# Where the second key head of the context is turned, and what ScalarE evicts around the scores

## The chip, the cores and the metric

The kernel runs on one core of one Trainium2 chip. The metric is the device time of one execution in microseconds (us). TensorE (PE) multiplies and also turns tiles by multiplying with an identity matrix, VectorE (DVE) reduces and normalises, ScalarE (ACT) evicts PSUM banks and takes exponentials, GpSimd (POOL) does elementwise work in SBUF, and SyncE (SP) issues the DMAs.

## The reference

One transformer block in float32 on `x` (8 batches of 112 tokens, 512 channels) with a context of 8 x 375 rows. The part that the change touches is the attention:

```python
ln_out = _ln(hidden_states, ln_w, ln_b)
q  = _ln(fp8_linear(ln_out, wq)).reshape(b, s, g, hpg, d)    # 16 heads, 8 key heads, d = 128
k  = _ln(fp8_linear(ln_out, wk)); v = fp8_linear(ln_out, wv)
core = _gqa(q, k, v)                                         # softmax(q k^T / sqrt(d)) v
qx = _ln(fp8_linear(ln_out, wqx))
kx, vx = split(einsum('bsi,oi->bso', cond, w_kv_x))          # cond: the context
kx = _ln(kx)
xout = _gqa(qx, kx, vx)                                      # 112 queries against 375 context rows
```

The two outputs are concatenated, quantised and projected, and a layer of experts follows, which the change does not touch.

## The kernel before

The weights of the projections are split into 4 groups (`GP`) of four query heads and two key heads. For each group the kernel goes over the 8 batches, so there are 32 attentions, numbered here t = 0 to 31. Each step of the order in `passes` (L399) projects a batch `s` and, interleaved with it, does the attention of the batch before it, `t`. Queries and own keys are projected for 128 rows at a time, so 7 of 8 batches carry such a tile ("has a tile") and the eighth only projects its own values and its context. The context of a batch is projected in three blocks of 125 rows, `project(s, 3)` to `project(s, 5)`, each 12 matmuls: four with the high halves `c_hi`, `w_hi`, four with `c_lo`, `w_hi`, four with `c_hi`, `w_lo`.

Every engine has its order written out by hand in a function `step`, and one called `last_step` for the batch without a tile. That gives five kinds of steps with an attention in them:

- plain steps, 20 of them (t = 4, 5, 8 to 13, 16 to 21, 24 to 29)
- steps that also round inputs on VectorE (`rounding`, L1043), 4 of them (t = 0 to 3, in the first group)
- last steps (`last_step`), 4 of them (t = 6, 14, 22, 30); in the first three VectorE also splits weights of the next group (`w_low`)
- first steps of a new group (`change == "new"`), 3 of them (t = 7, 15, 23)
- the attention of the last batch alone, 1 (t = 31)

A step in TensorE's order: the projections `project` 0 and 1, `turn` 0 to 2 (own queries, cross queries, own keys), `turn(t, 3)` (first key head of the context), `project` 2, `score_self`, `score_cross` 0 and 1, `turn(t, 4)` (second key head of the context), `project` 3, `turn_self` (L845), `turn_cross` 0 (L852), `score_cross` 2, `turn_cross` 1, `score_cross` 3, `project` 4, outputs, `turn_cross` 2 and 3, `project` 5, outputs. `turn_self` and `turn_cross` turn the probabilities; `turn_cross` 1 writes the PSUM bank that `turn_self` wrote, so it waits until VectorE has copied that bank out in `take_self` (L1121).

ScalarE: `c_high(s, k)` (L581) rounds a block of the context to `c_hi`; `turned(t, n)` (L640 for the context's keys) evicts a turned bank; `take(s, j)` evicts a projection; `exp_self` (L656) and `exp_cross` (L664) take the exponentials. GpSimd: `c_low(s, k)` (L529) computes `c_lo = c_raw - c_hi`, 128x500 float32 in SBUF, as soon as `c_high(s, k)` is done; `rstd(s, j)` (L516, L523) follows each. VectorE: `max_self` (L1093), `max_cross` (L1107), `norm_self` (L1101), `norm_cross` 0 and 1 (L1115, a tensor_scalar in SBUF), `take_self` (L1121), and later `scale(s, 5)` (L1087), which normalises the last block of the context's keys. SyncE reloads `c_raw` for block k when `c_high` and `c_low` of it are done.

Of the kernel before, what the change touches and what calls it, by code (L numbers as in the profile page):

```python
# [29 lines left out]
KB = D // P  # L30
# [197 lines left out]
def flat(ap):  # L228
    return ap.rearrange("p a b -> p (a b)")
# [7 lines left out]
def lin(pos):  # L237

    return B * pos[0] + pos[1]
# [52 lines left out]
def attention(nc, c, sb, ps, sem, x, vecs, scalars, smooth, ctxT, wproj, catd, vec, scal, gate,  # L292
# [265 lines left out]
    def _(act):  # L558
# [19 lines left out]
        def c_high(s, k):  # L578
            act.wait_ge(c_in_done[k], 16 * (lin(s) + 1))
            act.wait_ge(pj_rdy, pj_no(before(s), 3 + k))  # L580
            act.activation(flat(c_hi[:, k, :, :]), flat(c_raw[:, k, :, :]), ACT.Copy).then_inc(ch_done, 1)  # L581
# [48 lines left out]
        def turned(t, n):  # L630

            act.wait_ge(tr_rdy, tr_no(t, n))
            if n in (0, 2):
                act.wait_ge(ss_rdy, lin(t) + 1)
            else:
                act.wait_ge(sx_rdy, 4 * lin(t) + 4)
            w, b = ((V_QW, V_QB), (V_QXW, V_QXB), (V_KW, V_KB), (V_KXW, V_KXB), (V_KXW, V_KXB))[n]
            w, b = vec[:, w:w + 1], vec[:, b:b + 1]
            if n >= 3:
                act.activation(kxT[:, n - 3, :], turn_bank(n)[:, 0:TC], ACT.Identity, bias=b,  # L640
                               scale=w).then_inc(t_done, 1)
                return
            heads = (4, 4, 2)[n]
            src = turn_bank(n)[:, 0:heads * P].rearrange("p (h t) -> p h t", t=P)
            dst, u = (qT, qxT, kT)[n], t[1]
            own = T - (P - T) * u
            act.activation(dst[:, u % 2, :, T - own:T], src[:, :, 0:own], ACT.Identity, bias=b, scale=w)
            act.activation(dst[:, 1 - u % 2, :, 0:P - own], src[:, :, own:P], ACT.Identity, bias=b,
                           scale=w).then_inc(t_done, 1)
# [45 lines left out]
        def step(s, t, g, change, k):  # L695
            A, Q = s is not None and change != "first", t is not None
            Qt = Q and has_tile(t)
            if A and not has_tile(s):
                return last_step(s, t, g, change)
            if change == "new": w_high(g, 4, change)  # L700
            if Qt: turned(t, 0)
            if A: take(s, 0)
            if Qt: turned(t, 1)
            if Qt: turned(t, 2)
            if A: c_high(s, 0)
            if Q: turned(t, 3)
            if not A and Q: turned(t, 4)
            if A: take(s, 1)
            if A: c_high(s, 1)
            if Q: exp_self(t)  # L710
            if Q: exp_cross(t, 0)
            if Q: exp_cross(t, 1)
            if A and Q: turned(t, 4)
            if A: take(s, 2)
            if A: c_high(s, 2)
            if A: take(s, 3)
            if Q: exp_cross(t, 2)
            if Q: exp_cross(t, 3)
            if k is not None: weights.centre(act, g, k, 0)
            if change == "queries": w_high(g, 0, change)  # L720
            if A: take(s, 4)
            if k is not None: weights.centre(act, g, k, 1)
            if k is not None: weights.centre(act, g, k, 2)
            if change == "queries": w_high(g, 1, change)
            if A and s[1] == TJ - 1: c_high((s[0], B - 1), 0)
            if A: take(s, 5)
            if change == "first":
                c_high(s, 0)
                c_high(s, 1)
                act.wait_ge(tr_done, TJ)  # L730
                scaled_inputs(0)
                w_high(g, 4, change)
                c_high(s, 2)
                scaled_inputs(1)
                scaled_inputs(2)
                take(s, 3)
                scaled_inputs(3)
                take(s, 4)
                w_high(g, 0, change)
                take(s, 5)  # L740
                for n in range(1, 4):
                    w_high(g, n, change)
                for j in range(3):
                    take(s, j)
# [11 lines left out]
    def _(pe):  # L756
# [15 lines left out]
                              start=(i == 0), stop=(i == 2 * KB - 1))  # L772
            return m

        def project(s, j, g=None):

            pe.wait_ge(pj_done, pj_no(s, j) - (1 if j == 0 and s == (0, 1) else 2))
            bank = p_proj[:, j % 2, :]
            if j == 0 or not has_tile(s):
                pe.wait_ge(xqs_done, lin(s) + 1)  # L780
            if s == FIRST and j == 3:
                pe.wait_ge(y_done, 1)
            if j < 2:
                m = of_tokens(bank, j, P, (CQ, CQX)[j], 512, g, j)
            elif j == 2:
                if has_tile(s):
                    of_tokens(bank[:, 0:256], 2, P, CK, 256, g, 2)
                m = of_tokens(bank[0:T, 256:512], 3, T, CV, 256, g, 3)
            else:
                ch = j - 3  # L790
                if g is not None and ch == 0: pe.wait_ge(wh_done[4], g + 1)
                pe.wait_ge(ch_done, 3 * (lin(s) + 1) + ch + 1)
                for i in range(3 * KB):
                    k = i % KB
                    a, w = ((c_hi, w_hi), (c_lo, w_hi), (c_hi, w_lo))[i // KB]
                    if i == KB: pe.wait_ge(cl_done, 3 * (lin(s) + 1) + ch + 1)
                    if i == 2 * KB and g is not None and ch == 0: pe.wait_ge(wl_done[4], g + 1)
                    m = pe.matmul(bank[0:CT, :], a[:, ch, k, :], w[:, k, CKX:CV],  # L798
                                  start=(i == 0), stop=(i == 3 * KB - 1))
            m.then_inc(pj_rdy, 1)  # L800
# [14 lines left out]
        def turn(t, n):  # L815

            pe.wait_ge(ln_done, st_no(t, (0, 1, 2, 5, 5)[n]))
            bank_free(t, n)
            if n < 3:
                src = (nq, nqx, nk)[n]  # L820
                for h in range((4, 4, 2)[n]):
                    m = pe.transpose(turn_bank(n)[:, h * P:(h + 1) * P], src[:, h * P:(h + 1) * P], ident[:, :])
            else:
                for k in range(NC):
                    m = pe.transpose(turn_bank(n)[:, k * CT:(k + 1) * CT],
                                     nkx[0:CT, k, (n - 3) * P:(n - 2) * P], ident[0:CT, 0:CT])
            m.then_inc(tr_rdy, 1)
# [50 lines left out]
        def last_step(s, t):  # L878

            turn(t, 0)  # L880
            turn(t, 1)
            project(s, 2)
            turn(t, 2)
            project(s, 3)
            turn(t, 3)
            score_self(t)
            score_cross(t, 0)
            score_cross(t, 1)
            turn(t, 4)
            project(s, 4)  # L890
            turn_self(t)
            turn_cross(t, 0)
            score_cross(t, 2)
            turn_cross(t, 1)
            score_cross(t, 3)
            project(s, 5)
            turn_cross(t, 2)
            turn_cross(t, 3)
            outputs(t, 0)
            outputs(t, 1)  # L900

        def step(s, t, g, change, k):
            A, Q = s is not None, t is not None
            Qt = Q and has_tile(t)
            if A and not has_tile(s):
                return last_step(s, t)
            if change == "first":
                for j in (3, 4, 5, 0, 1, 2):
                    project(s, j, g)
                return  # L910
            if change != "new":
                g = None
            if A: project(s, 0, g)
            if Qt: turn(t, 0)
            if Qt: turn(t, 1)
            if A: project(s, 1, g)
            if Qt: turn(t, 2)
            if Q: turn(t, 3)
            if not A: turn(t, 4)
            if not A: score_self(t)  # L920
            if A: project(s, 2, g)
            if A and Q: score_self(t)
            if Q: score_cross(t, 0)
            if Q: score_cross(t, 1)
            if A and Q: turn(t, 4)
            if A: project(s, 3, g)
            if Q: turn_self(t)
            if Q: turn_cross(t, 0)
            if Q: score_cross(t, 2)
            if Q: turn_cross(t, 1)  # L930
            if Q: score_cross(t, 3)
            if A: project(s, 4)
            if Q: outputs(t, 0)
            if Q: turn_cross(t, 2)
            if Q: turn_cross(t, 3)
            if A: project(s, 5)
            if Q: outputs(t, 1)
# [1119 lines left out]
```

## Time and profile before

| | |
|---|---|
| median of 3 runs | 1150.24 us (1149.46 to 1151.94) |
| the profiled execution | 1153.25 us, span 1151.5 us |
| TensorE busy | 1092.3 us, 95% of the span |
| VectorE busy | 779.6 us, 68% |
| ScalarE busy | 698.5 us, 61% |
| GpSimd busy | 505.0 us, 44% |
| mean granted TensorE clock | 0.977 |

The attention runs until about 795 us of the span, the projection and the experts after it. The span is the time from the first to the last instruction; the time of the profiled execution is 1.75 us longer. "Busy" of TensorE counts matmuls whose modelled ends overlap the next one's start, so the spacing of starts tells more than durations.

### The profile page before, as it was taken

What the parts mean: (1) busy time and instruction counts of PE and PEld (TensorE: products, weight loads), DVE (VectorE), ACT (ScalarE), POOL (GpSimd) and SP (SyncE); (2) the same over time, 40 slices, a digit from 0 to 9 for tenths busy, and PEclk for the clock granted to TensorE, in tenths of its full rate; (3) what the DMA queues carried; (4) which work ended last, traced back from release to release, by engine and by line L of the source; (5) the groups of instructions that cost most, each with busy time, mean ns of one, the idle gap of its engine ahead of it and who ended that gap; (6) DMA issues with size and microseconds to landing.
All of it is one profiled execution on the core that took longest, in us unless ns stands there. A gap on an engine that the chain in (4) does not pass through costs nothing. (4 is left out here: it accounts for less than half of the span.)

```text
span 1151.5 us, 19576 instructions
## 1 busy us (share of the span) xinstructions
PE 1092.3 (95%) x5681; PEld 896.0 (78%) x5681; DVE 779.6 (68%) x1569; ACT 698.5 (61%) x2034; POOL 505.0 (44%) x576
## 2 busy tenths in 40 slices
PE   4599999999999999999999999998999789999996
PEld 3488788888888788888888888886888667777885
DVE  7998986977776887777697766677454884655000
ACT  7668878666878856888867656762231324334432
POOL 3445565445544454445544544542000225565432
PEclk8799999999999999999999999998999889999999
DMA  7221111142111214111114111112944347673220
GB/s 264 98 76 45 52 36 45 36 152 91 44 37 44 61 36 181 45 53 37 43 36 145 53 44 40 45 31 83 339 161 164 127 150 216 182 235 105 52 45 1
DMA packets 52820, 107.41 MB, mean 93 GB/s; under 512 B 6064, under 2 KB 27056, under 8 KB 51184
## 3 DMA queue, kind: packets, MB, share of 16 engines
q1 hardware_dynamic: 48016, 97.00, 25.7%
q0 software_dynamic: 4704, 9.18, 3.6%
q8 instruction: 50, 0.82, 0.3%
q14 instruction: 50, 0.41, 0.1%
HBM read 91.48 MB, written 16.52 MB: 94 GB/s over the span
## 5 line engine op out<-in xcount | busy, mean ns | idle before, releaser
L529 POOL TENSOR_TENSOR c_lo<-c_raw,c_hi 128x500 fp32r<-128x500 f32 x96 | 123.7, 1289 | 194.2 <-ACT c_hi L581 194.2
L523 POOL TENSOR_TENSOR rs<-va,mhalf 125x2 f32<-125x2 f32 (+1 forms) x180 | 200.7, 1115 | 14.2 <-POOL va L516 0.2
L516 POOL TENSOR_TENSOR va<-ss,epst 125x2 f32<-125x2 f32 (+1 forms) x180 | 60.6, 336 | 179.7 <-DVE ss L1078 101.5
L798 PE MATMUL bank<-w_hi,c_hi 128*125 128x512 f32 x384 | 120.0, 434 | 9.3 <-ACT w_hi L576 8.3
L771 PE MATMUL bank<-w_hi,xqs 128*128 128x512 f32 (+2 forms) x464 | 111.0, 361 | 11.4 <-DVE xqs L1070 11.4
L798 PE MATMUL bank<-w_lo,c_hi 128*125 128x512 f32 x384 | 105.4, 396 | 0.1
L798 PE MATMUL bank<-w_hi,c_lo 128*125 128x512 f32 x384 | 105.4, 396 | 0.0
L664 ACT ACTIVATE work<-bank,nmax 112x375 f32<-112x375 f32 x128 | 73.6, 584 | 46.7 <-DVE nmax L1107 46.7
L771 PE MATMUL bank<-w_lo,xqs 128*128 128x512 f32 (+2 forms) x464 | 101.0, 340 | 0.1
L842 PE MATMUL bank<-kxT,qxT 128*112 128x375 f32 x256 | 97.9, 484 | 0.0
L798 PEld LDWEIGHTS bank<-w_hi,c_hi 128*125 128x125 f32 x384 | 67.0, 188 | 27.6 <-issue 8.5
L771 PEld LDWEIGHTS bank<-w_hi,xqs 128*128 128x128 f32 (+1 forms) x464 | 73.7, 189 | 17.9 <-issue 12.0
L798 PEld LDWEIGHTS bank<-w_hi,c_lo 128*125 128x125 f32 x384 | 71.7, 187 | 18.5
L798 PEld LDWEIGHTS bank<-w_lo,c_hi 128*125 128x125 f32 x384 | 71.4, 186 | 18.8 <-DVE w_lo L434 0.8
L771 PEld LDWEIGHTS bank<-w_lo,xqs 128*128 128x128 f32 (+1 forms) x464 | 75.5, 187 | 11.4 <-DVE w_lo L434 0.8
L873 PE MATMUL bank<-work 125*128 125x224 f32 x384 | 83.2, 352 | 0.0
L1133 DVE TENSOR_TENSOR results<-bank,smg 128x448 bf16<-128x448 f32 x64 | 39.8, 622 | 53.2 <-PE bank L873 53.2
L626 ACT ACTIVATE nkx<-bank 125x256 f32<-125x256 f32 x96 | 38.8, 405 | 58.6 <-PE bank L798 58.6
L873 PEld LDWEIGHTS bank<-work 125*128 125x128 f32 x384 | 72.7, 190 | 0.4
L1107 DVE TENSOR_REDUCE nmax<-bank 112x1 f32<-112x375 f32 x128 | 69.1, 542 | 4.0 <-PE bank L842 1.3
L1523 POOL DMA_INDIRECT out<-p_cat,of_row x21 | 45.5, 2167 | 58.5 <-ACT p_cat L1627 43.4
L856 PEld LDWEIGHTS bank<-ident,work 112*125 112x125 f32 x384 | 52.2, 189 | 19.5 <-issue 13.6
(274 smaller groups left out, 2812.6 us busy)
## 6 DMA issues: line engine op xcount, KB each, us to landing
c_raw<-in_ctxT SPq DMA_DIRECT2D x96, 250.0 KB, 2.6
shared<-in_w_in SPq DMA_DIRECT2D x13, 1024.0 KB, 9.1
shared<-in_wproj SPq DMA_DIRECT2D x32, 256.0 KB, 4.5
raw_g<-in_Wg SPq DMA_DIRECT2D x8, 1024.0 KB, 6.5
raw_u<-in_Wu SPq DMA_DIRECT2D x8, 1024.0 KB, 6.1
raw_d<-in_Wd SPq DMA_DIRECT2D x8, 1024.0 KB, 5.5
cat_scratch<-results SPq DMA_DIRECT2D x32, 224.0 KB, 2.0
shared<-cat_scratch SPq DMA_DIRECT2D x2, 1792.0 KB, 9.0
```

The source lines that it names most:

```text
L516: pool.tensor_tensor(va[0:rows, lo:hi], ss[0:rows, lo:hi], epst[0:rows, lo:hi], ALU.add).then_inc(va_done, 1)
L523: pool.tensor_tensor(rs[0:rows, lo:hi], va[0:rows, lo:hi], mhalf[0:rows, lo:hi], ALU.pow).then_inc(rs_done, 1)
L529: pool.tensor_tensor(flat(c_lo[:, k, :, :]), flat(c_raw[:, k, :, :]), flat(c_hi[:, k, :, :]).bitcast(F32), ALU.subtract).then_inc(cl_done, 1)
L664: act.activation(pcross[0:T, h, :], p_cross[0:T, h % 2, 0:TC], ACT.Exp, bias=nmax[0:T, 4 + h:5 + h], accum_out=lsum[0:T, 4 + h:5 + h]).the ...
L771: m = pe.matmul(out, xqs[:, n, k, 0:rows], (w_hi, w_lo)[i // KB][:, k, lo:lo + w], start=(i == 0), stop=(i == 2 * KB - 1))
L798: m = pe.matmul(bank[0:CT, :], a[:, ch, k, :], w[:, k, CKX:CV], start=(i == 0), stop=(i == 3 * KB - 1))
L842: pe.matmul(p_cross[0:T, h % 2, 0:TC], qxT[:, t[1] % 2, h, :], kxT[:, h // HPG, :], start=True, stop=True).then_inc(sx_rdy, 1)
L856: m = pe.transpose(p_tr[0:CT, 1 - h % 2, k * T:(k + 1) * T], pcross[0:T, h, k * CT:(k + 1) * CT], ident[0:T, 0:T])
L873: m = pe.matmul(out[:, HPG * T:2 * HPG * T], valx[0:CT, par, k, g * P:(g + 1) * P], flat(pcrossT[0:CT, k, HPG * g:HPG * (g + 1), :]), star ...
L1107: v.tensor_reduce(nmax[0:T, 4 + h:5 + h], p_cross[0:T, h % 2, 0:TC], AX, ALU.max, negate=True).then_inc(mx_done, 1)
L1133: v.tensor_tensor(results.y[lin(t) % 2][:, g * 4 * T:(g + 1) * 4 * T].rearrange("p (a t) -> p a t", t=T), out_bank(t, g)[:, 0:4 * T].rearr ...
L1523: pool.indirect_dma_start(out=tokens[:, :], out_offset=bass.IndirectOffsetOnAxis(ap=of_row[:, 1, i:i + 1], axis=0), in_=y[:, i % 2, :], in ...
```

## The change

In `step`, TensorE turns the second key head of the context (`turn(t, 4)`) before `score_self` instead of after `score_cross` 1, in plain, rounding and new steps alike. ScalarE evicts it (`turned(t, 4)`) before `exp_self` instead of after `exp_cross` 1, and `c_high(s, 1)` takes the place behind `exp_cross` 1. In `last_step`, TensorE turns the first key head (`turn(t, 3)`) inside `project(s, 3)`, after its first four matmuls, instead of after all twelve; the orders of the other engines stay in that step.

```diff
@@ ScalarE, step
             if A: take(s, 1)
-            if A: c_high(s, 1)
+            if A and Q: turned(t, 4)
             if Q: exp_self(t)
             if Q: exp_cross(t, 0)
             if Q: exp_cross(t, 1)
-            if A and Q: turned(t, 4)
+            if A: c_high(s, 1)
             if A: take(s, 2)
@@ TensorE
-        def project(s, j, g=None):
+        def project(s, j, g=None, t=None):
@@
                     a, w = ((c_hi, w_hi), (c_lo, w_hi), (c_hi, w_lo))[i // KB]
+                    if i == KB and t is not None: turn(t, 3)
                     if i == KB: pe.wait_ge(cl_done, 3 * (lin(s) + 1) + ch + 1)
@@ TensorE, last_step
             turn(t, 2)
-            project(s, 3)
-            turn(t, 3)
+            project(s, 3, None, t)
             score_self(t)
@@ TensorE, step
             if A: project(s, 2, g)
+            if A and Q: turn(t, 4)
             if A and Q: score_self(t)
             if Q: score_cross(t, 0)
             if Q: score_cross(t, 1)
-            if A and Q: turn(t, 4)
             if A: project(s, 3, g)
```

## Rows read from the trace of the kernel before

**Rows 1.** Page, part 1: busy us, share of the span, instructions.

```profile
PE 1092.3 (95%) x5681; PEld 896.0 (78%) x5681; DVE 779.6 (68%) x1569; ACT 698.5 (61%) x2034; POOL 505.0 (44%) x576
```

**Rows 2.** Waits of PE, whole span: us in total, times, longest.

```profile
PE bank L856 <- DVE pselfT L1121: 2.8, 7, 0.5
```

**Rows 3.** Timeline, plain step (t = 10): start us, us, engine, line, operation, count [idle before].

```profile
301.40 0.63 DVE L1093 TENSOR_REDUCE nmax<-bank 112x4 f32<-112x448 f32 x1 [2.02 <-PE bank L835]
...
302.53 1.26 POOL L529 TENSOR_TENSOR c_lo<-c_raw,c_hi 128x500 fp32r<-128x500 f32 x1
...
304.49 0.69 ACT L640 ACTIVATE kxT<-bank,vec 128x375 f32<-128x375 f32 x1
...
304.85 0.74 DVE L1115 TENSOR_SCALAR work<-work,linv 112x375 f32<-112x375 f32 x2
...
306.15 0.62 DVE L1121 COPY pselfT<-bank 112x448 f32<-112x448 f32 x1 [0.56 <-PE bank L849]
...
306.28 0.80 PE L842 MATMUL bank<-kxT,qxT 128*112 128x375 f32 x2
...
306.93 0.55 PE L856 MATMUL bank<-ident,work 112*125 112x112 f32 x3
```

**Rows 4.** Timelines, last step of the last group (t = 30), the normalising of probabilities.

```profile
771.71 0.64 ACT L581 ACTIVATE c_hi<-c_raw 128x500 fp32r<-128x500 f32 x1
...
772.07 1.83 DVE L1115 TENSOR_SCALAR work<-work,linv 112x375 f32<-112x375 f32 x2
...
772.43 1.26 POOL L529 TENSOR_TENSOR c_lo<-c_raw,c_hi 128x500 fp32r<-128x500 f32 x1 [4.55 <-ACT c_hi L581]
...
773.82 0.61 DVE L1121 COPY pselfT<-bank 112x448 f32<-112x448 f32 x1
```

**Rows 5.** The same, a narrow window: the second of the two L1115 alone.

```profile
772.40 1.50 DVE L1115 TENSOR_SCALAR work<-work,linv 112x375 f32<-112x375 f32 x1
```

**Rows 6.** Timeline, step with rounding (t = 1).

```profile
90.95 0.95 DVE L1053 TENSOR_SCALAR re<-xq 128x1024 uint16<-128x1024 uint16 x1
...
92.31 0.69 ACT L640 ACTIVATE kxT<-bank,vec 128x375 f32<-128x375 f32 x1
...
93.22 0.74 DVE L1115 TENSOR_SCALAR work<-work,linv 112x375 f32<-112x375 f32 x2
...
93.88 0.68 DVE L1057 TENSOR_TENSOR xq<-xq,re 128x1024 bf16<-128x1024 bf16 x1
...
94.48 0.62 DVE L1121 COPY pselfT<-bank 112x448 f32<-112x448 f32 x1
...
95.24 0.55 PE L856 MATMUL bank<-ident,work 112*125 112x112 f32 x3 [0.34 <-DVE pselfT L1121]
```

**Rows 7.** Instructions of L1053: duration ns min/median/max, first and last start.

```profile
L1053 DVE TENSOR_SCALAR re<-xq x14: 407/424/1033, 36.2 to 152.9; 128x1024 uint16<-128x1024 uint16 x14
```

**Rows 8.** Timeline, first step of a new group (t = 7).

```profile
233.25 0.69 ACT L640 ACTIVATE kxT<-bank,vec 128x375 f32<-128x375 f32 x1
...
234.58 0.62 DVE L1121 COPY pselfT<-bank 112x448 f32<-112x448 f32 x1
...
235.44 0.48 PE L856 MATMUL bank<-ident,work 112*125 112x112 f32 x3
```

**Rows 9.** Timeline, last step of the first group (t = 6), around project 3.

```profile
204.89 1.08 PE L798 MATMUL bank<-w_hi,c_lo 128*125 128x512 f32 x4
...
205.19 0.42 DVE L1087 TENSOR_TENSOR nkx<-nkx,rs 125x256 f32<-125x256 f32 x1
...
206.74 0.48 PE L825 MATMUL bank<-ident,nkx 125*128 125x125 f32 x3
...
207.06 0.95 PE L835 MATMUL bank<-kT,qT 128*112 128x112 f32 x8
...
207.98 1.51 PE L842 MATMUL bank<-kxT,qxT 128*112 128x375 f32 x4
```

**Rows 10.** The same step, later: the two L1115 of `norm_cross` 0 and 1.

```profile
212.12 1.74 DVE L1115 TENSOR_SCALAR work<-work,linv 112x375 f32<-112x375 f32 x2
```

## The prediction

> **What bounds the kernel now.** I read the page first: TensorE is busy 95% of the span [rows 1]. Then TensorE's list of waits: in the attention it hardly waits, the entry that bears on this change being `turn_cross`, which waited 7 times, 2.8 us in all, for VectorE's copy `take_self` [rows 2]. Last the timeline of one step of each kind. A step of the attention is therefore a queue of TensorE work with no gap, and moving TensorE work about gains nothing by itself. What can move the time is a wait that opens. The reader should look at `turn_cross` 1, because it is the only place with no reserve. In the plain step it starts at 306.93; the score before it starts at 306.28 as two matmuls 0.31 apart (half the 0.63 from 306.28 to 306.91), so the engine is free at 306.91, and `take_self` ends at 306.77, after which PE needs 0.15 (in the rounding step 94.48 + 0.62 = 95.10, PE starts at 95.24) [rows 3, 6]. So 306.92 against 306.91: both releasers arrive together. Every delay of `take_self` is paid in full by TensorE.
>
> **The scores start later.** Turning one key head takes 0.32 us of TensorE (turn 3 at 206.74, next work at 207.06) [rows 9]. Moved ahead of the scores, it costs TensorE nothing, since `project` 3 still starts at the same time, but `score_self` and all behind it on VectorE and ScalarE come 0.32 later. In the plain step VectorE waited 2.02 us for the scores [rows 3], so nothing upstream absorbs this. ScalarE is on time: `turned(t, 4)` takes the slot of `c_high(s, 1)`, both 0.64 to 0.69 us long [rows 3, 4]. Downstream `take_self` had 0.56 us of idle ahead of it [rows 3], so by this alone 0.24 would be left and the plain step would lose nothing.
>
> **`c_high(s, 1)` behind `exp_cross` 1: the main term.** `c_high` releases `c_low` on GpSimd. Before, `c_low(s, 1)` ran at 302.53 to 303.79, ahead of the two `norm_cross` at 304.85 [rows 3]. Afterwards its releaser starts where `turned(t, 4)` starts now. The last steps already have just this order (`exp_cross` 1, then `c_high(s, 2)`), so they show what happens. In t = 30, counted from the start of `c_high`: first L1115 at +0.36, second at +0.69, `c_low` at +0.72, and the second L1115 takes 1.50 us; the pair takes 1.83 where it takes 0.74 in the plain step, 0.41 each at a spacing of 0.33; `take_self` comes at +2.11 [rows 3, 4, 5]. The plain step has the same distance: ScalarE's next instruction at 304.49, L1115 at 304.85, +0.36 [rows 3]. So VectorE will be blocked there too. `take_self` then starts at 304.49 + 0.32 + 2.11 = 306.92 instead of 306.15, ends at 307.53, and TensorE starts `turn_cross` 1 at 307.68 instead of 306.93: 0.75 us. Twenty plain steps: 15.0 us. The bounds of this term are 0 (VectorE keeps its port and GpSimd waits) and 1.09 us (the whole stretch, 1.83 - 0.74 [rows 3, 4]) per step, 0 to 21.8 us; I take 0.75 because t = 30 repeats the distances within 0.01 us.
>
> The Trainium skill ("SBUF — State Buffer", section "Who interferes with whom") says that VectorE in a two-port mode, tensor_scalar among the operations that can enter it, and GpSimd exclude each other, and that the one that issues first gets the ports for its whole instruction. In t = 30 the second L1115 is recorded 0.03 us before `c_low` and is nevertheless the one that waits; taken by recorded starts alone, that rule gives the plain steps no loss, which is the first rival below.
>
> **Steps with rounding (4).** The same move, but here `take_self` is already late: TensorE idled 0.34 us [rows 6]. The L1053 of `rounding` takes 0.95 beside `c_low(s, 1)` and 0.42 by the median [rows 6, 7]; with `c_low` gone it gives 0.52 back, against the 0.32 of the later scores. The L1115 stand 0.91 behind ScalarE's next instruction (93.22 - 92.31); less the 0.52 they come at +0.39 and +0.72, and `c_low` at +0.72: a near tie, which t = 30 (+0.69 against +0.72) decides for GpSimd. With the second blocked, VectorE is free for the rest of `rounding` at +2.11, and this takes 0.60 (L1057 at 93.88, `take_self` at 94.48 [rows 6]). `take_self` is then at 92.31 + 0.32 + 2.11 + 0.60 = 95.34 instead of 94.48: 0.86 us, four times, 3.4 us. Bounds: -0.2 (the relief alone) and 1.1 per step.
>
> **New groups (3).** VectorE is behind here and the later scores are absorbed. `c_low` comes at 233.25 + 0.72 = 233.97. VectorE's own order keeps the L1115 some 0.6 us behind `c_high`, so the first is under way and the second blocked, as in t = 6, where the pair took 1.74 us [rows 10]. With +2.17 (an estimate: the 2.11 of t = 30 and a little for the later L1115) `take_self` comes at 235.42, ends 236.04, TensorE starts at 236.19 instead of 235.44 [rows 8]: 0.75, three times, 2.2 us. Bounds 0 and 1.1.
>
> **Turn 3 inside `project` 3 (4 last steps).** It removes nothing, it moves three turns up by eight matmuls. But a turn waits for `scale(s, 5)` of the step before. In t = 6 this L1087 ends at 205.61, because VectorE splits weights before it; the slot of the turn is now at 204.89 [rows 9]. All of TensorE, the eight matmuls of `project` 3 first, then the scores, queues behind it until 205.61 + 0.15 = 205.76: 0.87 us, of which I take 0.16 off, the gap that the scores had until now behind the late eviction (0.92 from 207.06 to 207.98 for 0.76 of work; an estimate from the spacing of 0.095 of its eight matmuls). That is 0.7, three times, 2.1 us. Bounds 0 (VectorE's later work in that step is late anyway) and 0.87. In t = 30 no weights are split, the turn isn't late, and `take_self` still sets `turn_cross` 1: 0.
>
> **What is moved past, and costs nothing.** `c_low(s, 1)` ends at 304.81 + 0.72 + 1.26 = 306.79; the next GpSimd work, `rstd(s, 1)`, waits for `sums(s, 1)`, which stands behind `take_self` (306.92) on VectorE. `project` 4 needs `c_hi` of block 1 at its start, after 307.6, and has it at 305.5. The reload of `c_raw` block 1 on SP's queue starts some 3 us later for a use 20 us away; what is queued behind it, block 2's reload, waits for a `c_low` that is later still. `take(s, 2)` shifts by the 0.3 only. If GpSimd's cover went, `rstd(s, 1)` and with it `scale(s, 1)` would come later, and these have until the next step's turns.
>
> Sum: 15.0 + 3.4 + 2.2 + 2.1 = 22.7 us. The profiled execution (1153.25 us, span 1151.5) lies 3.0 above the median of the runs; it would become 1176.0, and the median 1150.24 + 22.7 = 1172.9.
>
> **The rivals.**
> 1. VectorE keeps the port. The second L1115 is recorded 0.03 us ahead of `c_low` [rows 4, 5]; if the grant goes to it in the plain steps, GpSimd waits 0.4 us and nobody is late. The point from which it decides: L1115 granted before `c_low`, 0.03 to 0.1 us either way. Then plain steps give 0, rounding steps -0.2 each (-0.8), new groups -0.1 each (-0.4), last steps +2.1: 1151.1. Against it: t = 30, and t = 6, where L1115 is later still and also blocked [rows 10]. Chance 0.08, of which I put 0.05 within 0.2% (2.3 us, about what a measurement of this kernel can tell from no change).
> 2. The same, and turn 3 isn't late either, since the L1087 before it is earlier against TensorE than read. Then only the reliefs are left, with the 0.16 gap of four last steps closed: -0.8 - 0.4 - 0.6 = -1.8, or up to -2.6 with the late copy fully relieved in the rounding steps (0.34 each instead of 0.2): 1147.6. Chance 0.03 in all, counted as faster.
> 3. Both L1115 are blocked, `c_low` coming before the first. Then `turn_cross` 0 waits as well, about 1.1 us per plain step (the whole stretch): 22 + 3.4 + 2.2 + 2.1 = 30, 1180. It needs `c_low` 0.35 us earlier than t = 30 shows. Chance 0.05.
> 4. The change does what it says, the key head is ready before the second pair of scores, but `score_cross` 2 never waited for it (no wait of L842 on ScalarE stands in the list that rows 2 are from). So no rival on the faster side comes from the aim itself.
>
> **How the numbers follow.** Forecast 0.82, rival 1 at 0.08, rival 2 at 0.03, rival 3 at 0.05, other slower cases 0.02. The forecast's own range: plain steps 0.65 to 0.85 (13 to 17), rounding steps 2.4 to 4.0, new groups 1.2 to 2.7, last steps 1.0 to 2.8, together 18 to 26.5: 1168 to 1177. With 1.5 us of spread between medians it is 1166 to 1178, and that leaves out less than 2 in 10. Faster 0.03, within 0.2% 0.05, slower 0.92.
>
> **What would show it.** In the changed profile: twenty L1115 near 1.5 us that were 0.41 in plain steps, L529 within 0.1 us of them; `turn_cross` 1 waiting for L1121 in nearly every step, some 0.75 us each, where rows 2 show 7 waits; L1053 of the rounding steps back at 0.42; `project` 3 of t = 6, 14, 22 with a hole of 0.8 us ahead of the turn; plain steps of 24.6 us instead of 23.85. It would be wrong if L529 is the long one (above 1.6 us) and L1115 stays at 0.41.

## The result

| | before | after |
|---|---|---|
| median | 1150.14 us (1149.46 to 1151.94, 4 runs) | 1164.52 us (1163.21 to 1165.90, 4 runs) |
| profiled execution: span | 1151.5 us | 1161.4 us |
| mean granted TensorE clock | 0.977 | 0.982 |

The ratio is 1.0123 with a 95% interval of 1.0108 to 1.0138: slower by 14.4 us. The prediction was 1172.9 us with a range of 1166 to 1178, so the direction was right and the time lies below the range.

The spans differ by less than the medians (9.9 us). The windows tell why: from the end of the attention on, the profiled execution of before had a lower granted clock for a stretch, the changed one had not. Columns: stretch, its length, busy us of each engine, granted clock, DMA share, GB/s. First before, then after, each the last 17 to 18 us of the attention and the 41 to 43 us behind it:

```profile
779.00:797.00 18.00, 14.87 (x72) 11.30 (x71) 11.28 (x26) 5.86 (x23) 0.89 (x2) 0.91 0.00 0
797.00:840.00 43.00, 40.82 (x173) 33.73 (x174) 23.20 (x40) 11.18 (x19) 5.47 (x17) 0.96 0.87 305
```

```profile
792.00:809.00 17.00, 13.57 (x73) 10.22 (x72) 11.38 (x26) 5.98 (x24) 0.89 (x2) 1.00 0.00 0
809.00:850.00 41.00, 38.93 (x172) 32.25 (x173) 22.65 (x40) 10.97 (x18) 5.48 (x17) 1.00 0.92 320
```

So I compare the attentions up to the end of t = 30, ahead of that stretch. TensorE's last matmul of its outputs starts at 781.88 us before and at 794.99 after: 13.1 us. Step by step, the distance between the ends of the outputs of successive attentions grew as follows:

| steps | each | sum |
|---|---|---|
| plain, second L1115 stretched: 13 of 20 | +0.73 to +0.77 | +9.7 |
| plain, spared: 7 of 20 (t = 5, 9, 13, ... 29) | +0.01 to +0.02 | +0.1 |
| with rounding, 4 | -0.53, then -0.19 to -0.21 | -1.1 |
| first of a group, 3 | +0.80 to +0.81 | +2.4 |
| last, 3 with split weights, and t = 30 | +0.65 to +0.67; +0.05 | +2.0 |

The -0.53 is that of t = 0, which also holds the start of the kernel.

The page after has GpSimd's and VectorE's lines for the two sides of the collision, L529 at a mean of 1339 ns (1289 before) and L1115 at 597, and TensorE's waits say where it is paid: `turn_cross` (now L857) waited 17 times for `take_self`, where [rows 2] had 7. The 17 are the 13 plain steps, the three new ones and t = 30. An idle time shown behind a matmul is some 0.16 us too short, because the modelled end of that matmul lies later than the start that the next one could have: 0.58 shown goes with 0.75 lost.

```profile
L529 POOL TENSOR_TENSOR c_lo<-c_raw,c_hi 128x500 fp32r<-128x500 f32 x96 | 128.5, 1339 | 275.3 <-ACT c_hi L581 275.3
...
L1115 DVE TENSOR_SCALAR work<-work,linv 112x375 f32<-112x375 f32 x128 | 71.1, 597 | 2.2
```

```profile
PE bank L857 <- DVE pselfT L1121: 10.1, 17, 0.7
...
PE bank L857 <- DVE work L1115: 2.1, 4, 0.6
PE bank L826 <- DVE nkx L1087: 1.8, 3, 0.6
```

A plain step that lost (t = 10), timeline of the changed kernel; it answers to [rows 3]:

```profile
306.69 0.64 ACT L581 ACTIVATE c_hi<-c_raw 128x500 fp32r<-128x500 f32 x1
...
307.06 1.82 DVE L1115 TENSOR_SCALAR work<-work,linv 112x375 f32<-112x375 f32 x2
...
307.41 1.25 POOL L529 TENSOR_TENSOR c_lo<-c_raw,c_hi 128x500 fp32r<-128x500 f32 x1 [2.95 <-ACT c_hi L581]
...
308.80 0.61 DVE L1121 COPY pselfT<-bank 112x448 f32<-112x448 f32 x1
...
309.56 0.55 PE L857 MATMUL bank<-ident,work 112*125 112x112 f32 x3 [0.58 <-DVE pselfT L1121]
```

The distances are those of t = 30 of before: L1115 at +0.37, `c_low` at +0.72, `take_self` at +2.11 from `c_high`. And a plain step that was spared (t = 9), the same view:

```profile
282.82 0.65 ACT L581 ACTIVATE c_hi<-c_raw 128x500 fp32r<-128x500 f32 x1
...
283.19 0.74 DVE L1115 TENSOR_SCALAR work<-work,linv 112x375 f32<-112x375 f32 x2
...
283.55 1.50 POOL L529 TENSOR_TENSOR c_lo<-c_raw,c_hi 128x500 fp32r<-128x500 f32 x1 [2.96 <-ACT c_hi L581]
...
284.18 0.62 DVE L1121 COPY pselfT<-bank 112x448 f32<-112x448 f32 x1 [0.25 <-PE bank L850]
...
284.95 0.55 PE L857 MATMUL bank<-ident,work 112*125 112x112 f32 x3
```

Counted from the start of `c_high`, the starts are the same to 0.01 us, but here GpSimd waits: L529 takes 1.50 instead of 1.25, the pair of L1115 0.74, and TensorE starts the turn when it is free. The 0.25 of idle ahead of L1121 is the reserve of 0.24 that the prediction had left.

The rounding step (t = 1) answers to [rows 6]:

```profile
90.75 0.42 DVE L1053 TENSOR_SCALAR re<-xq 128x1024 uint16<-128x1024 uint16 x1
...
92.49 0.74 DVE L1115 TENSOR_SCALAR work<-work,linv 112x375 f32<-112x375 f32 x2
...
92.84 2.10 POOL L529 TENSOR_TENSOR c_lo<-c_raw,c_hi 128x500 fp32r<-128x500 f32 x1 [2.97 <-ACT c_hi L581]
...
93.14 0.69 DVE L1057 TENSOR_TENSOR xq<-xq,re 128x1024 bf16<-128x1024 bf16 x1
```

VectorE won here four times out of four, and `c_low` waited not only for the second L1115 but for the L1057 behind it as well: 2.10 us. It ends at 94.94, 1.11 us behind the end of L1057 at 93.83; in the spared plain step it ends 1.11 us behind the end of the second L1115.

The last step (t = 6) answers to [rows 9]; the hole stands ahead of the turn and its releaser is the one predicted:

```profile
203.52 1.18 PE L799 MATMUL bank<-w_hi,c_hi 128*125 128x512 f32 x4
...
204.83 0.42 DVE L1087 TENSOR_TENSOR nkx<-nkx,rs 125x256 f32<-125x256 f32 x1
...
205.30 0.54 PE L826 MATMUL bank<-ident,nkx 125*128 125x125 f32 x3 [0.60 <-DVE nkx L1087]
...
212.38 1.75 DVE L1115 TENSOR_SCALAR work<-work,linv 112x375 f32<-112x375 f32 x2
...
213.86 0.58 PE L857 MATMUL bank<-ident,work 112*125 112x112 f32 x3 [0.62 <-DVE work L1115]
```

The last two lines show something that the prediction did not have: `c_low` now starts 0.05 us ahead of the first L1115 in t = 6, 14 and 22, and the first is the stretched one (1.41 to 1.43 us, the second 0.40). `turn_cross` 0 waits for it, where before `turn_cross` 1 waited for `take_self`.

### The profile page after: what moved, and what is told of

Same layout as the page of the kernel before. It is cut to its first block and busy times, and to the rows that moved or that the text cites. A ratio compares the mean times of both kernels' runs of the same rounds, so it can differ in the third digit from the quotient of the medians.

```text
span 1161.4 us, 19576 instructions
## 1 busy us (share of the span) xinstructions
PE 1091.1 (94%) x5681; PEld 894.2 (77%) x5681; DVE 793.6 (68%) x1569; ACT 699.3 (60%) x2034; POOL 508.2 (44%) x576
## 5 line engine op out<-in xcount | busy, mean ns | idle before, releaser
L529 POOL TENSOR_TENSOR c_lo<-c_raw,c_hi 128x500 fp32r<-128x500 f32 x96 | 128.5, 1339 | 275.3 <-ACT c_hi L581 275.3
L523 POOL TENSOR_TENSOR rs<-va,mhalf 125x2 f32<-125x2 f32 (+1 forms) x180 | 202.1, 1123 | 14.2 <-POOL va L516 0.2
L799 PE MATMUL bank<-w_hi,c_hi 128*125 128x512 f32 x384 | 125.7, 449 | 7.5 <-ACT w_hi L576 6.7
L857 PEld LDWEIGHTS bank<-ident,work 112*125 112x125 f32 x384 | 51.8, 188 | 31.4 <-DVE work L1115 23.5
L1115 DVE TENSOR_SCALAR work<-work,linv 112x375 f32<-112x375 f32 x128 | 71.1, 597 | 2.2
L857 PE MATMUL bank<-ident,work 112*125 112x112 f32 x384 | 59.5, 277 | 12.8 <-DVE pselfT L1121 10.1
```

The source lines that it names most:

```text
L523: pool.tensor_tensor(rs[0:rows, lo:hi], va[0:rows, lo:hi], mhalf[0:rows, lo:hi], ALU.pow).then_inc(rs_done, 1)
L529: pool.tensor_tensor(flat(c_lo[:, k, :, :]), flat(c_raw[:, k, :, :]), flat(c_hi[:, k, :, :]).bitcast(F32), ALU.subtract).then_inc(cl_done, 1)
L857: m = pe.transpose(p_tr[0:CT, 1 - h % 2, k * T:(k + 1) * T], pcross[0:T, h, k * CT:(k + 1) * CT], ident[0:T, 0:T])
L1115: v.tensor_scalar(pcross[0:T, h, :], pcross[0:T, h, :], linv[0:T, 4 + h:5 + h], None, ALU.mult).then_inc(nx_done, 1)
```

## The experiments

The theory: GpSimd's `c_low(s, 1)` and VectorE's second `norm_cross` want one port at the same instant; who gets it first is a tie within some 20 ns, and each step that VectorE loses costs TensorE 0.75 us. The rivals: the later scores cost the time and the stretched instruction only goes with them; or the spared steps are spared for another reason. Each experiment names its median against the runs of before on the same chip; "in the attention" is the shift of the end of t = 30 against before, as above. Each program left one profiled execution. The step t = 0 with the start of the kernel was between 1.76 us shorter and 0.14 longer in them than before, so every such shift carries that much of it, and what is said of "each" step leaves t = 0 out.

**The second L1115 a little later.** The changed kernel, with one tiny VectorE instruction:

```diff
             if Q: norm_cross(t, 0)
+            if Q: v.memset(pad[:, 0:1], 0.0)
             if Q: norm_cross(t, 1)
```

> The changed kernel with one tiny VectorE instruction (a memset of one column) between the two norm_cross of every plain, rounding and new step. It delays the second L1115 by some 60 to 100 ns, nothing else. Theory (a tie for the port): in the changed kernel the second L1115 is recorded 18 to 24 ns ahead of c_low and lost 13 of 20 plain steps and 0 of 4 rounding steps; now it is recorded behind c_low and must lose 20 of 20 and 4 of 4, so 7 x 0.75 + 4 x 1.07 = 9.5 us are added to 1164.5: about 1174 us. Rival (the loss comes from the later scores and the order of TensorE, the stretched L1115 only accompanies it): no more than the instruction itself, 1164.5 to 1166 us, and the same 13 stretched.

Measured: 1168.81 us (1.0146, 1.0126 to 1.0166), in the attention 19.3 us. The memset moved the second L1115 by some 10 ns only in the record, from 18 to 24 ns ahead of `c_low` to 4 to 16 ns. All 20 plain steps are stretched, but of the rounding steps only t = 0 and 2 (there +0.85 in the step against -0.2). My 1174 asked for four. For the plain steps this run shows little: the changed kernel without the memset lost 18 of them in another execution (below), with a median of 1168.0 us, so the 1168.8 do not refute the rival either. What the memset does show is that a rounding step can be lost too; in the two profiled executions of the changed kernel none was. A memset of 128 columns, meant to move L1115 further, did not fit into SBUF beside the kernel's tensors and has no time.

**`c_low` a little later.** The changed kernel, with one tiny ScalarE instruction:

```diff
             if Q: exp_cross(t, 1)
+            if A and Q: act.activation(pad[:, 1:2], vec[:, 0:1], ACT.Copy)
             if A: c_high(s, 1)
```

> The changed kernel with one tiny ScalarE instruction (one column) ahead of c_high(s, 1), which delays c_low by 0.1 to 0.2 us. Theory (a tie for the port): VectorE wins all 20 plain steps, L1115 stays at 0.41, and c_low takes 1.5 us or less; 13 x 0.75 = 9.7 us go away from 1164.5: 1154.8; if the second L1115 of the three new steps is also freed, 2.4 less: 1152.4. Rival (later scores and TensorE order): 1164.5, or a little more, since c_low comes later still.

Measured: 1153.77 us (1.0025, 1.0013 to 1.0038), in the attention 2.6 us. It moves `c_low` by 0.09 us, and all 20 plain steps are as long as before, within 0.02 us. The third plain attention of the second group, timeline (the lines moved by two):

```profile
304.50 0.64 ACT L582 ACTIVATE c_hi<-c_raw 128x500 fp32r<-128x500 f32 x1
...
304.77 0.74 DVE L1117 TENSOR_SCALAR work<-work,linv 112x375 f32<-112x375 f32 x2
...
305.22 1.41 POOL L530 TENSOR_TENSOR c_lo<-c_raw,c_hi 128x500 fp32r<-128x500 f32 x1 [3.07 <-ACT c_hi L582]
...
305.76 0.62 DVE L1123 COPY pselfT<-bank 112x448 f32<-112x448 f32 x1 [0.25 <-PE bank L852]
```

An added instruction thus makes the kernel 11 us faster than without it. The scores are as late as in the changed kernel, so their lateness costs nothing. The three new steps are still stretched (0.81 each); there the second L1115 is later, 18 to 25 ns behind `c_low`, and all three lose.

**Turn 3 alone.** Before, with the last-step part of the diff and nothing else.

> The kernel before with the last-step part alone (turn 3 inside project 3). Theory: three holes of about 0.6 us ahead of the turn in t = 6, 14, 22, where it waits for the nkx of L1087, none in t = 30: 1150.1 + 2.0 = 1152.1 us. Rival (the stall is absorbed, since VectorE is behind in that step anyway): 1150.1 us, with the hole ahead of the turn but turn_cross 1 where it was.

Measured: 1152.90 us (1.0020, 1.0006 to 1.0034); the steps t = 6, 14 and 22 are 0.61, 0.63 and 0.63 longer, t = 30 by 0.07, all others by 0.01 or less. The three holes stand in TensorE's waits:

```profile
PE bank L826 <- DVE nkx L1087: 1.8, 3, 0.6
```

**The same turn four matmuls later.** Before, with `if i == 2 * KB and t is not None: turn(t, 3)` instead of `i == KB`.

> The kernel before with turn 3 inside project 3 of the last steps, but after eight of the twelve matmuls instead of four. Theory (the 0.63 us a step of the last-step part is the wait for the nkx of L1087 and nothing else): its slot is now at about 205.8, the nkx is there at 205.61, no hole ahead of the turn, t = 6, 14 and 22 as long as before or up to 0.1 shorter: 1150.1 us. Rival (a turn between the matmuls of one block costs by itself): the 0.6 us a step of the variant with four stay.

Measured: 1149.60 us (1.0005, 0.9992 to 1.0018); the three steps are 0.08 to 0.09 shorter than before. The loss of this part is the wait for `scale(s, 5)` and not the turn in the midst of a block. Timeline of TensorE, t = 6, no idle ahead of the turn:

```profile
204.63 1.07 PE L799 MATMUL bank<-w_hi,c_lo 128*125 128x512 f32 x4
205.54 0.48 PE L826 MATMUL bank<-ident,nkx 125*128 125x125 f32 x3
```

**Turn 4 alone, on TensorE.** Before, with TensorE's `turn(t, 4)` ahead of `score_self`; ScalarE's order is that of before.

> The kernel before with turn 4 ahead of the scores on TensorE alone; ScalarE's order stays, so c_high(s, 1) and c_low(s, 1) stay where they were. Theory: plain and new steps lose nothing (0.56 us of idle ahead of take_self covers the 0.32), the four rounding steps lose 0.32 each, since take_self is late there already: 1150.1 + 1.3 = 1151.4 us, no stretched L1115 but those of the last steps. Rival (the later scores are what costs the 0.75 us): 20 x 0.3 to 0.75 us more, 1157 to 1165 us.

Measured: 1150.18 us (0.9993, 0.9982 to 1.0005). No step differs from before by more than 0.03 us (t = 30: 0.06), the rounding steps neither, where I had expected 0.32 each. The timeline of t = 1, GpSimd's and VectorE's lines, shows why:

```profile
90.32 1.26 POOL L529 TENSOR_TENSOR c_lo<-c_raw,c_hi 128x500 fp32r<-128x500 f32 x1
91.22 0.64 DVE L1053 TENSOR_SCALAR re<-xq 128x1024 uint16<-128x1024 uint16 x1
91.89 0.43 DVE L1055 TENSOR_SCALAR re<-re 128x1024 uint16<-128x1024 uint16 x1
```

L1053 took 0.95 us in [rows 6] and ended 0.28 us behind `c_low`. Begun 0.3 later, it again ends 0.28 behind `c_low` (91.86 against 91.58) and takes 0.64. This stretched instruction absorbs the lateness ahead of it.

**`c_high(s, 1)` alone.** Before, with only this:

```diff
-            if A: c_high(s, 1)
             if Q: exp_self(t)
             if Q: exp_cross(t, 0)
             if Q: exp_cross(t, 1)
+            if A: c_high(s, 1)
             if A and Q: turned(t, 4)
```

> The kernel before with c_high(s, 1) moved behind exp_cross 1, ahead of turned(t, 4), and nothing else: the scores are not later, TensorE's order is that of before. Theory (the moved c_low is the whole loss): the second L1115 is stretched in most or all plain steps. Where it is, take_self comes at 304.39 + 2.21 = 306.60 instead of 306.15, so 0.32 less late than in the changed kernel: 0.43 us a step instead of 0.75. With 13 of 20 blocked 5.6 us, with 20 of 20 8.6; new steps 0.8 x 3 = 2.4; rounding steps -0.3 each where spared: 1150.5 + 7 to 10 = 1157 to 1161 us. Rival (moving TensorE's turn is needed for the loss): 1150.5 us.

Measured: 1160.24 us (1.0087, 1.0068 to 1.0105), in the attention 7.6 us. All 20 plain steps stretched, 0.39 to 0.44 each; new steps 0.79 to 0.80; rounding steps spared, -0.48 to -0.49. The move of one ScalarE instruction, with nothing changed on TensorE, brings the collision. What turn 4 adds is the 0.32 by which the reserve ahead of `take_self` is smaller: 0.43 becomes 0.75.

**The changed kernel once more.**

> The changed kernel once more, to see whether the outcome of the tie is a property of the program or of the execution. Theory A (the outcome is set by the phase at which the program arrives, the same each time): the second L1115 is stretched in the same 13 of 20 plain steps, t = 5, 9, 13, 17, 21, 25 and 29 being spared, and in none of the four rounding steps; about 1164.5 us. Theory B (it differs from execution to execution): another number of stretched ones, each worth 0.75 us.

Measured: 1168.01 us (1165.85 to 1170.25, 4 runs; 1.0157, 1.0135 to 1.0179), in the attention 15.9 us. The same program, and now 18 of 20 plain steps are stretched; t = 5 and t = 25 are spared, t = 9 is not:

```profile
282.76 1.49 DVE L1115 TENSOR_SCALAR work<-work,linv 112x375 f32<-112x375 f32 x1
284.18 0.61 DVE L1121 COPY pselfT<-bank 112x448 f32<-112x448 f32 x1
```

So theory B holds between two profiled executions. They come from two separate sets of four runs (1163.21 to 1165.90 and 1165.85 to 1170.25 us), so whether the outcome changes from one execution to the next or only from set to set, a chip for instance, is not shown.

The recorded distance doesn't tell who wins: at 23 and 24 ns both outcomes occur in plain steps. Nor is the tie at the same distance in every kind of step. Plain steps lost at 10 to 26 ns; rounding steps were spared at 17 to 21 ns in both executions of the changed kernel and at 5 to 15 ns in `c_high(s, 1)` alone, 12 of 12, and with the memset they lost at 4 ns and won at 7; t = 30 lost at 21 to 25 ns in all ten profiled executions that keep its order and its tensor_scalar. The 3.5 us between the medians of 1164.5 and 1168.0 for one kernel is about what five steps of 0.75 come to, and by five stretched steps the profiled executions differ.

**The second L1115 clearly later.** The changed kernel, with a small reduce that nobody reads:

```diff
             if Q: norm_cross(t, 0)
+            if Q: v.tensor_reduce(pad[:, :], vec[:, 0:NV].unsqueeze(1).to_broadcast([P, 4, NV]), AX, ALU.add)
             if Q: norm_cross(t, 1)
```

> The changed kernel with a small independent VectorE reduce (128 elements read, 4 written, a sum that nobody uses) between the two norm_cross of every step but the last ones. It puts the second norm_cross clearly behind the start of c_low. Theory (a tie for the port, decided within some 20 ns): 20 of 20 plain steps and 4 of 4 rounding steps are stretched; in the attention 20 x 0.75 + 4 x 0.85 + 3 x 0.8 + 3 x 0.64 = 22.7 us more than before, the sum that was predicted blind: about 1172 us. Rival (the rounding steps are spared for a reason other than the tie): 15 + 2.4 + 1.9 - 0.8 = 18.5, 1168 us.

Measured: 1173.12 us (1.0213, 1.0189 to 1.0237). All 20 plain steps (0.71 to 0.76) and all 4 rounding steps are stretched (t = 1 to 3: 0.84 to 0.85). In the attention 21.1 us; the 1.6 below my 22.7 are mostly t = 0, -0.35 where 0.85 was expected, the step that also holds the start of the kernel. The rounding step t = 1, timeline:

```profile
93.02 1.25 POOL L530 TENSOR_TENSOR c_lo<-c_raw,c_hi 128x500 fp32r<-128x500 f32 x1 [2.98 <-ACT c_hi L582]
...
93.20 1.28 DVE L1116 TENSOR_SCALAR work<-work,linv 112x375 f32<-112x375 f32 x1
...
95.01 0.61 DVE L1122 COPY pselfT<-bank 112x448 f32<-112x448 f32 x1
...
95.76 0.55 PE L858 MATMUL bank<-ident,work 112*125 112x112 f32 x3 [1.19 <-DVE pselfT L1122]
```

**Another instruction for the same product.** The changed kernel:

```diff
-            v.tensor_scalar(pcross[0:T, h, :], pcross[0:T, h, :], linv[0:T, 4 + h:5 + h], None, ALU.mult)
+            v.tensor_tensor(pcross[0:T, h, :], pcross[0:T, h, :],
+                            linv[0:T, 4 + h:5 + h].to_broadcast([T, TC]), ALU.mult)
```

> The changed kernel with the tensor_scalar of norm_cross written as a tensor_tensor with the factor broadcast along the row: the same result, two inputs from SBUF instead of one and a scalar. By norm_self (0.62 for 448 columns) it takes 0.52 instead of 0.41, so the second is issued about 0.1 us behind c_low. Theory 1 (two inputs from SBUF want the same port, as the Trainium skill says in SBUF — State Buffer, Who interferes with whom): the second is stretched in all 20 plain and 4 rounding steps, 1172 us. Theory 2 (only the tensor_scalar's fast mode wants the port): none is stretched, take_self waits for nothing new in the plain steps, 1150.5 + 3.5 = 1154 us, and 1 to 2 us more from 0.2 us a step where VectorE is late.

Measured: 1181.44 us (1.0282, 1.0260 to 1.0304). Theory 1 holds: the second is stretched to 1.6 us in every plain and rounding step. The size was off, 0.97 to 1.01 a plain step instead of 0.75: an unhindered one takes 0.55 instead of 0.41, and the stretched one ends 0.41 us behind `c_low` instead of 0.21. Durations in ns, min, median and max, of all 128:

```profile
L1115 DVE TENSOR_TENSOR work<-work,linv x128: 535/550/1620, 67.7 to 823.7; 112x375 f32<-112x375 f32 x128
```

The Trainium skill ("SBUF — State Buffer", section "Who interferes with whom") says that a VectorE instruction with two inputs in SBUF contends with a GpSimd instruction that reads SBUF; this run agrees, and so does L1057 above. The rule that the one that issues first gets the ports agrees wherever the recorded distance is 0.09 us or more, and wherever `c_low` is recorded first (18 to 25 ns in the new steps of the run with the ScalarE instruction); it can't be read from recorded starts where L1115 is 0.02 ahead.

**No collision at all.** Before, with ScalarE's order changed so that no `c_low` falls on these two instructions:

```diff
 ScalarE, step
-            if A: c_high(s, 1)
             if Q: exp_self(t)
             if Q: exp_cross(t, 0)
             if Q: exp_cross(t, 1)
             if A and Q: turned(t, 4)
             if A: take(s, 2)
+            if A: c_high(s, 1)
             if A: c_high(s, 2)
 ScalarE, last_step
-            c_high(s, 2)
             turned(t, 4)
             take(s, 3)
+            c_high(s, 2)
```

> The kernel before with ScalarE's order alone changed so that no c_low falls on the two norm_cross: c_high(s, 1) behind take(s, 2) in step, and c_high(s, 2) behind take(s, 3) in last_step. Turn 3 and turn 4 stay where they were. Theory (each c_low beside a VectorE instruction that wants the port is worth what TensorE waits there): no stretched L1115 at all, L1053 of the rounding steps at 0.42, TensorE's wait of 0.34 gone in four rounding steps (-1.3 us), of 0.47 in three and 0.2 in one last step (-1.6), 0.17 less in three new steps (-0.5): 1150.5 - 3.4 = 1147.1 us. Rival (c_low falls on another VectorE instruction and takes as much): 1150.5 us or more.

Measured: 1147.28 us over 11 runs against 1149.50 (0.9971, 0.9960 to 0.9982, which is 2.1 to 4.6 us): faster than both kernels. In the attention -4.2 us, at the upper end of that: rounding steps t = 1 to 3 -0.48 to -0.49 each, which makes them as long as plain ones, last steps -0.64 and t = 30 -0.14, new steps -0.17, plain steps 0.00. No L1115 is stretched, and L1053 has lost its long ones (max 1033 ns in [rows 7]):

```profile
L1053 DVE TENSOR_SCALAR re<-xq x14: 411/417/428, 35.8 to 151.6; 128x1024 uint16<-128x1024 uint16 x14
```

## Why the prediction was wrong in size

**Right: what bounds the kernel and the mechanism.** `turn_cross` 1 had no reserve, moving TensorE work alone did nothing (turn 4 alone: 1150.18), the moved `c_high(s, 1)` brings `c_low` onto the second L1115, and a stretched one costs 0.75 us (measured 0.73 to 0.77).

**Wrong: "So VectorE will be blocked there too".** This is the step that failed. The distances of one instance, t = 30, were taken as deciding for 20 plain steps. The second L1115 was recorded 0.03 us ahead of `c_low` there. t = 30 itself loses every time, but equal recorded distances did not carry its outcome over to the plain steps: in the profiled execution 13 of 20 were lost, in the second one 18. The term of 15.0 us measured 9.8.

**Wrong for the same reason: the rounding steps.** I called it "a near tie, which t = 30 decides for GpSimd". It went the other way four times in each of the two profiled executions of the changed kernel: predicted +3.4, measured -1.1, of which -0.53 is t = 0. The bound of -0.2 that I gave as the relief alone was the value of t = 1 to 3.

**Small terms.** New groups: 2.2 predicted, 2.4 measured. Turn 3: 2.1 predicted, 2.0 measured (the three steps alone 1.9), with t = 30 near zero (0.05); the sign, the place and the releaser held. With turn 3 alone the turn starts 0.77 us behind its slot (0.87 predicted) and `score_cross` 0.69 later (0.7 predicted). How it goes on from there was not in the prediction: the stretch passes to the first L1115.

**Sum.** The predicted sum of 22.7 us is that of a kernel that loses every tie. Where the tie was forced, it came out: 1173.12 us (1170.42 to 1175.87) against 1172.9. The kernel that wins them in plain and rounding steps has 1153.77, 2.7 us above the 1151.1 of rival 1. That difference is the new groups, which I had put at -0.4 and which stayed stretched at +2.4. The changed kernel lies between these two, and where it lies differs from one set of runs to another: 1164.52 is below the range of 1166 to 1178, the second median of the same program, 1168.01, inside it. What was wrong in the reckoning was to give 0.82 to one end and 0.08 to the other where the evidence was a single row at 0.03 us, and to place the lower end of the range at 1166 instead of carrying the bound of 0 per step, stated in the text, into it. The expectation of 0.32 for the later scores in rounding steps was also wrong (turn 4 alone: at most 0.03), because L1053 ended 0.28 us behind `c_low` whichever of the two times it began.

**Open.** What decides the tie inside some 20 ns isn't settled, nor why it tips at about 24 ns in plain steps and about 5 ns in rounding steps. Two executions of one program gave different sets of lost steps with the same recorded starts to a few ns, and every fourth plain step being spared in the first of them points to a phase between the engines; that is argued, not shown.

## What to carry to other kernels

When an order on one engine is changed, look at what its results release on the others: here a ScalarE instruction moved by 3.5 us cost nothing on ScalarE, and 12.1 of the 14.2 us that steps lost came from the GpSimd instruction that it releases. Read GpSimd's instructions against VectorE's line by line, and treat a distance under 0.1 us between two that want one port as a tie: carry both outcomes into the range, or move one of them by 0.1 us and have the outcome fixed. A duration that varies in a group (0.42 and 0.95, 0.41 and 1.50) marked such a collision in this kernel, and taking it away was worth more here than any move of TensorE's work.

## What the runs showed that I had not expected

An unused instruction of ScalarE (0.23 us in the record, `c_low` 0.09 us later) makes the changed kernel 11 us faster, and a VectorE memset of one column that moves a start by 10 ns goes with 7 more lost plain steps of 20 and a median 4 us higher, though the same program without it also lost 18 in another execution. One program has medians of 1164.5 and 1168.0 us in two sets of four runs, and the five further lost ties of the second profiled execution would come to about that (its attention is 2.8 us longer, 3.6 without t = 0); the granted clock of the two was about the same (0.982 and 0.979). A GpSimd instruction that loses can be held through two VectorE instructions in a row (2.10 us for 1.25 of work), the second of them a tensor_tensor that itself isn't stretched (0.69).
